# Reading the relative-position tables two units ahead, in pairs of batches

## The reference, cut to what matters

```python
q, k, v = heads(x @ Wq + bq), heads(x @ Wk + bk), heads(x @ Wv + bv)
pos_k = heads(rel_embeddings @ Wk + bk)              # 128 distance buckets
scores = q @ k.T
scores += take(q @ pos_k.T, bucket(i - j))           # c2p
scores += take(k @ pos_k.T, bucket(j - i)).T         # p2c
ctx = softmax(scores / sqrt(48)) @ v
out = layernorm(ctx @ Wo + bo + x) * ln_scale + ln_bias
```

## Time and profile before

| | us |
|---|---|
| median of 3 runs | 2724.37 (2719.42 to 2726.56) |
| the profiled execution's own time | 2727.48 |
| its span, first to last instruction | 2725.4 |
| granted TensorE clock, mean of the span | 0.847 of full |
| PE busy | 1965.8 (72%) |
| DVE busy | 1632.0 (60%) |
| ACT busy | 1046.4 (38%) |
| POOL busy | 898.0 (33%) |
| DMA, queue 1 (SP's) packets | 269344 packets, 398.77 MB |

### The profile page before, as it was taken

The page is one execution under the profiler, slowest core; times in us unless marked ns, Lnnn a source line. Parts: engine busy times, 40 slices in busy tenths (PEclk is TensorE's granted clock), DMA queues, the critical chain, the costliest instruction groups (busy, mean ns, idle before and its releaser), DMA issues. The chain is left out here.

```text
span 2725.4 us, 47318 instructions
## 1 busy us (share of the span) xinstructions
PE 1965.8 (72%) x13556; PEld 1445.9 (53%) x13557; DVE 1632.0 (60%) x4103; ACT 1046.4 (38%) x2098; POOL 898.0 (33%) x1079
## 2 busy tenths in 40 slices
PE   6867777777777777777769999755335159999742
PEld 3435666666666666665646666433225028877421
DVE  8946665666666566665765553577747754444344
ACT  3445554555555555555423223332001163333000
POOL 4122222222222222222232220267630015554656
PEclk9979898998988888888979999777565559999876
DMA  4679998998999899999742110000001414447333
GB/s 149 195 238 287 278 290 262 290 280 271 284 266 281 255 281 269 276 280 282 233 122 62 48 30 1 0 0 0 0 19 47 178 32 155 154 148 139 109 97 110
DMA packets 290039, 456.40 MB, mean 167 GB/s; under 512 B 38608, under 2 KB 225024, under 8 KB 289824
## 3 DMA queue, kind: packets, MB, share of 16 engines
q1 hardware_dynamic: 269344, 398.77, 48.6%
q0 software_dynamic: 16320, 42.39, 6.3%
q10 hardware_dynamic: 4160, 12.58, 1.2%
HBM read 236.67 MB, written 216.92 MB: 166 GB/s over the span
## 5 line engine op out<-in xcount | busy, mean ns | idle before, releaser
L935 DVE CUSTOM_DVE_ANT_0 probs<-bank,c2p 128x512 f32<-128x512 f32 x512 | 351.8, 687 | 425.7 <-PE bank L832 217.9
L893 ACT ACTIVATE probs<-probs,neg_max 128x512 f32<-128x512 f32 x512 | 371.5, 726 | 69.9 <-DVE neg_max L935 69.5
L908 ACT COPY a_stage<-bank 128x320 f32<-128x320 f32 (+1 forms) x512 | 211.9, 414 | 427.1 <-PE bank L801 416.3
L944 DVE COPY probsT<-bank 128x512 f32<-128x512 f32 x512 | 351.2, 686 | 11.0 <-PE bank L842 10.6
L842 PE MATMUL bank<-ident,probs 128*128 128x128 f32 x2048 | 334.7, 289 | 1.0 <-ACT probs L893 0.9
L813 PE MATMUL bank<-tab,k 96*128 96x320 bf16 (+1 forms) x512 | 165.0, 322 | 197.1 <-DVE b_stage L887 149.6
L842 PEld LDWEIGHTS bank<-ident,probs 128*128 128x128 f32 x2048 | 277.3, 152 | 13.1 <-issue 1.8
L771 POOL COPY end_c2p<-a_stage 128x4 f32<-128x4 f32 (+1 forms) x128 | 24.8, 194 | 752.0 <-ACT a_stage L908 596.9
L2122 POOL DMA_INDIRECT p_x_tile<-y_d,p_token x160 | 153.0, 956 | 329.4 <-POOLq L1813 207.4
L832 PE MATMUL bank<-ident,p2c 128*128 128x128 f32 x1280 | 249.1, 296 | 0.0
L827 PE MATMUL bank<-k,q 96*128 96x384 bf16 (+1 forms) x512 | 167.3, 327 | 91.7 <-DMA p2c<-p2c_d 66.2
(11 more groups left out here) (254 smaller groups left out, 3770.0 us busy)
## 6 DMA issues: line engine op xcount, KB each, us to landing
p2c_d<-b_stage SPq DMA_DIRECT2D x64, 640.0 KB, 4.9
c2p_d<-a_stage SPq DMA_DIRECT2D x64, 640.0 KB, 4.5
p2c_d<-b_stage SPq DMA_DIRECT2D x64, 576.0 KB, 5.2
c2p_d<-a_stage SPq DMA_DIRECT2D x64, 576.0 KB, 3.5
p2c<-p2c_d SPq DMA_DIRECT2D x256, 144.0 KB, 4.5
c2p<-c2p_d SPq DMA_DIRECT2D x256, 144.0 KB, 4.3
o_sorted_d<-p_o_pair SPq DMA_DIRECT2D x80, 256.0 KB
k<-k_stack_d SPq DMA_DIRECT2D x192, 64.0 KB
```

Source lines behind the costliest of these rows:

```text
L893: act.activation(probs[:, w % 2, j, :], probs[:, w % 2, j, :], ACT.Exp, bias=neg_max[:, w % 2, j:j + 1], scale=-1.0).then_inc(exp_done, 1)
L908: act.copy(staged(a_stage, wa % 2, wa % TPB)[:, j, :], bank[A_BANK][:, 0:width(wa % TPB)]).then_inc(a_copied, 1)
L935: dve.tensor_tensor_reduce(probs[:, w % 2, j, :], bank[S_BANKS[(HB * w + j) % 3]][:], c2p[:, w % 2, j, :], -SCALE, LOWEST, ALU.add, ALU.mi ...
L944: dve.tensor_copy(probsT[:, wp % 2, j], bank[T_BANKS[j % 2]][:].rearrange("p (k q) -> p k q", k=TPB)).then_inc(probsT_copied, 1)
```

## The change

The tables' four sequences are stored as two pairs (r) with the two members (e) of a pair alternating element by element, in the stage buffers, in HBM, and in the c2p and p2c tiles: [b, x] becomes [r, x, e]. A skewed read then takes runs of 320 to 576 floats, half as many. The copies into the stage buffers write every second element, DVE's add and PE's stationary load read every second element, and POOL's fills write pairs. c2p gets four buffers; its reads are issued directly behind the p2c reads of the same unit, two units ahead, and A_LEAD becomes 4. POOL's c2p fill waits for the adds of a unit one earlier. SP waits, ahead of the write of table A, for the c2p read of four units before. To make room, rows3, w1 and the second half of the row sums are no longer held beside stage 2: they are loaded at the start of stage 3, with waits there.

```diff
-        rsum_in = sb(early3, "p3_rsum", [P, 2, CC, S], side="right")
+        first_sums = sb(early3, "p3_first_sums", [P, CC, S], side="right")
...
-        w1 = sb(early3, "p3_w1", [P, CC, FFN], side="right")
-        rows3 = sb(early3, "p3_rows", [P, 4, C], side="right")
...
-        A_LEAD, B_LEAD = 3, 4
+        A_LEAD, B_LEAD = 4, 4
...
-            return stage[:, u, 0:HB * width(t)].rearrange("p (b x) -> p b x", b=HB)
+            return stage[:, u, 0:HB * width(t)].rearrange("p (r x e) -> p r x e", r=HB // 2, e=2)
...
-            c2p = sb(st, "c2p", [P, 2, HB, S])
+            c2p = sb(st, "c2p", [P, TPB, HB // 2, S, 2])
-            p2c = sb(st, "p2c", [P, TPB, HB, NEAR])
+            p2c = sb(st, "p2c", [P, TPB, HB // 2, NEAR, 2])
...
+            WEIGHTS3 = [(wo[:], a["wo"].rearrange("(c p) n -> p c n", p=P)), (b1[:], a["b1_col"]), (scale[:], row("scale"))]
...
                     def read_skewed(table_d, slot, t, dest, left, done):
                         for g in range(P // ROWS):
                             j0, j1 = varied(t, g)
-                            start = slot * P * HB * TABLE + ROWS * g * HB * width(t) + ROWS - 1 - ROWS * g - first_col(t)
-                            skew = bass.AP(table_d.tensor, start + j0,
-                                           [[HB * width(t) - 1, ROWS], [width(t), HB], [1, j1 - j0]])
-                            sp.dma_start(dest[g * ROWS:(g + 1) * ROWS, :, j0 + left:j1 + left], skew).then_inc(done, 16)
+                            start = slot * P * HB * TABLE + ROWS * g * HB * width(t) + 2 * (ROWS - 1 - ROWS * g - first_col(t))
+                            skew = bass.AP(table_d.tensor, start + 2 * j0,
+                                           [[HB * width(t) - 2, ROWS], [2 * width(t), HB // 2], [1, 2 * (j1 - j0)]])
+                            sp.dma_start(dest[g * ROWS:(g + 1) * ROWS, :, j0 + left:j1 + left, :]
+                                         .rearrange("p r x e -> p r (x e)"), skew).then_inc(done, 16)
...
-                        (i2, w2), (i1, w1) = ahead(i, w, 2), ahead(i, w, 1)
+                        i2, w2 = ahead(i, w, 2)
                         if is_unit(i2, w2):
-                            kt = w2 % TPB
+                            t = w2 % TPB
                             sp.wait_ge(b_written[w2 % 2], 16 * (BODY // 2 * i2 + w2 // 2 + 1))
                             apart(sp)
                             sp.wait_ge(p2c_filled, BODY * i2 + w2 + 1)
-                            read_skewed(p2c_d, kt, kt, p2c[:, kt], 0, p2c_loaded[kt])
-                        if is_unit(i1, w1):
-                            t = w1 % TPB
-                            sp.wait_ge(a_written[w1 % 2], 16 * (BODY // 2 * i1 + w1 // 2 + 1))
+                            read_skewed(p2c_d, t, t, p2c[:, t], 0, p2c_loaded[t])
+                            sp.wait_ge(a_written[w2 % 2], 16 * (BODY // 2 * i2 + w2 // 2 + 1))
                             apart(sp)
-                            sp.wait_ge(c2p_filled, BODY * i1 + w1 + 1)
-                            read_skewed(c2p_d, w1 % 4, t, c2p[:, w1 % 2], (t - 1) * P, c2p_loaded[w1 % 2])
+                            sp.wait_ge(c2p_filled, BODY * i2 + w2 + 1)
+                            read_skewed(c2p_d, t, t, c2p[:, t], (t - 1) * P, c2p_loaded[t])
...
                         if is_unit(ia, wa):
+                            wait_count(sp, c2p_loaded[wa % TPB], 64 * (4 * ia + wa // TPB))
...
-                            return pool.tensor_copy(dest[:, :, c0:c1], ends_of[:, side, :].unsqueeze(2).broadcast_to(
-                                [P, HB, c1 - c0]))
+                            pairs = ends_of[:, side, :].rearrange("p (r e) -> p r e", e=2)
+                            return pool.tensor_copy(dest[:, :, c0:c1, :],
+                                                    pairs.unsqueeze(2).broadcast_to([P, HB // 2, c1 - c0, 2]))
...
-                            wait_count(pool, scores_added, HB * n)
-                            pool.wait_ge(a_ends_copied, BODY * i1 + w1 + 1)
+                            left = (t - 1) * P
+                            wait_count(pool, scores_added, HB * (n - 1))
+                            pool.wait_ge(a_ends_copied, BODY * i2 + w2 + 1)
...
-                            last = pe.matmul(sc[:, kt * P:(kt + 1) * P], p2c[:, kt, j, (t - kt + 1) * P:(t - kt + 2) * P],
+                            last = pe.matmul(sc[:, kt * P:(kt + 1) * P], p2c[:, kt, j // 2, (t - kt + 1) * P:(t - kt + 2) * P, j % 2],
...
-                    copy(staged(b_stage, w % 2, w % TPB)[:, j, :], bank[B_BANK][:, 0:width(w % TPB)]).then_inc(copied, 1)
+                    copy(staged(b_stage, w % 2, w % TPB)[:, j // 2, :, j % 2], bank[B_BANK][:, 0:width(w % TPB)]).then_inc(copied, 1)
...
-                                    probs[:, w % 2, j, :], bank[S_BANKS[(HB * w + j) % 3]][:], c2p[:, w % 2, j, :],
+                                    probs[:, w % 2, j, :], bank[S_BANKS[(HB * w + j) % 3]][:], c2p[:, w % TPB, j // 2, :, j % 2],
...
+                    sp.dma_start(rows3[:, 0, :], row("bo")).then_inc(rows_loaded, 16)
                     load_in(0, 0)
+                    for k, name in ((1, "ln_scale"), (2, "ln_bias"), (3, "b2")):
+                        sp.dma_start(rows3[:, k, :], row(name)).then_inc(rows_loaded, 16)
+                    for c in range(CC):
+                        heads = slice(c * H // CC, (c + 1) * H // CC)
+                        sp.dma_start(rsum_in[:, 1, c], ctx_d[heads, 1:2, D:2 * D, :].rearrange("h b d s -> h (b d) s")
+                                     ).then_inc(next_loaded, 16)
                     sp.dma_start(sums[:], ctx_d[:, :, D, :]).then_inc(sums_loaded, 16)
+                    sp.dma_start(w1[:], a["w1T"].rearrange("(c p) n -> p c n", p=P)).then_inc(w1_loaded, 16)
...
+                        if isinstance(b, int) and b == 0:
+                            pool.wait_ge(rows_loaded, 16 * 4)
                         pool.tensor_tensor(n_bo[:], n_in[:, u], across(0), ALU.add).then_inc(n_bo_ready, 1)
...
+                        if isinstance(b, int) and b == 0:
+                            dve.wait_ge(w1_loaded, 16)
```

More of the change, by code:

```diff
@@ L614, in build @@
             a_written = [sem("a_written0"), sem("a_written1")]
-            c2p_loaded = [sem("c2p_loaded0"), sem("c2p_loaded1")]
+            c2p_loaded = [sem(f"c2p_loaded{k}") for k in range(TPB)]
             b_made = sem("b_made")
@@ L722, in step @@
                                     heads = slice(c * H // CC, (c + 1) * H // CC)
-                                    for dest, rows in ((ctx_in, slice(0, D)), (rsum_in, slice(D, 2 * D))):
-                                        sp.dma_start(dest[:, u, c], ctx_d[heads, u:u + 1, rows, :]
+                                    for dest, rows in ((ctx_in[:, u, c], slice(0, D)), (first_sums[:, c], slice(D, 2 * D)))[:2 - u]:
+                                        sp.dma_start(dest, ctx_d[heads, u:u + 1, rows, :]
                                                      .rearrange("h b d s -> h (b d) s")).then_inc(first_ctx_loaded[u], 16)
@@ L728, in _ @@
                         sp.wait_ge(ctx_written[g], 16 * UNITS // TPB // 2)
-                    sp.wait_ge(first_ctx_loaded[1], 16 * 2 * CC)
+                    sp.wait_ge(first_ctx_loaded[1], 16 * CC)
                 @block.gpsimd
@@ L754, in step @@
                             last.then_inc(p2c_filled, 1)
-                        if is_unit(i1, w1):
-                            t, left = w1 % TPB, (w1 % TPB - 1) * P
-                            lo, hi = near_tiles(t)
-                            wait_count(pool, scores_added, HB * n)
-                            pool.wait_ge(a_ends_copied, BODY * i1 + w1 + 1)
+                            left = (t - 1) * P
+                            wait_count(pool, scores_added, HB * (n - 1))
+                            pool.wait_ge(a_ends_copied, BODY * i2 + w2 + 1)
                             apart(pool)
                             for side, c0, c1 in constant(t):
-                                last = fill(c2p[:, w1 % 2], end_c2p[:, w1 % 4], side,
+                                last = fill(c2p[:, t], end_c2p[:, t], side,
                                             0 if side == 0 else c0 + left, S if side else c1 + left)
@@ L770, in copy_ends @@
                             apart(pool)
-                            pool.tensor_copy(ends_of[:, w % 4, ends(t), :].rearrange("p s b -> p b s"),
-                                             staged(stage, w % 2, t)[:, :, end_cols(t)]).then_inc(copied, 1)
+                            pool.tensor_copy(ends_of[:, w % 4, ends(t), :].rearrange("p s (r e) -> p r s e", e=2),
+                                             staged(stage, w % 2, t)[:, :, end_cols(t), :]).then_inc(copied, 1)
                         if is_unit(ia, wa):
@@ L907, in step @@
                                     wait_count(act, a_ends_copied, m - 1)
```

(11 more changed lines are left out.)

9 lines of the change are left out of this document (3 added, 6 removed).

## The result

The changed kernel takes 2762.68 us (median of 4 runs, 2758.16 to 2763.08) against 2725.47 for the kernel before in the same session: ratio 1.0132, interval 1.0105 to 1.0159. It is slower by 1.3%, where 2.2% faster was forecast (60 us). Its profiled execution has a span of 2756.4 us, 31.0 more than before.

A forecast was written before the change was run, and what follows sets the result against it. Stage 2 was taken to be bound by DMA transfers, lateness costing time only through DMA gaps. Terms of -43, -12, -4 and -1 sum to -60 us: 2667.5 for the profiled execution, 2664 against the median, range 2585 to 2712.

The forecast's parts named there:

- term 1: Stage 2, c2p read two units ahead: DVE's 176.2 us wait goes and DMA gaps close, -43 us.
- At nothing: Parts of the change counted as 0 us: A_LEAD 4, SP's new wait, POOL's fills, strided operands and PE's stationary load.
- a sign of being wrong: Stage 2's DMA share staying at 0.94 or below, where 0.97 or more was to show the forecast right.
- The best window of 100 us: Stage 2's fastest of eleven windows, taken as its pace with gaps closed: 8.82 us per unit for 9.16.
- the wait only changes its name: Rival, stage 2: p2c, loop ends and the b_stage copy hold DVE instead, share stays 0.94; 2708 us, chance 0.12.
- Term 2: Stage 2's table reads: half as many packets of twice the length read 2% faster, -12 us.
- The strong rival: Packet length matters strongly for stage 2's reads, which reach about 290 GB/s; 2600 us, chance 0.27.
- The estimate of 14 us: Stage 2's reads: 512 fewer packets per unit at a fixed three cycles each, 0.11 us per unit.
- Term 3: Loads moved to stage 3: -5.5 us from stage 2's last loop body, +1.5 at stage 3's start, net -4.
- The slow rival: PE's stationary load from p2c at 8-byte steps costs double, deciding from 64 ns more a load; 2799 us, chance 0.10.
- The 0 for ACT's strided copy: Stage 2: strided operands were taken to cost DVE and ACT nothing, 0 us.

The follow-up runs named there:

- j_early_loads: The change with every quarter of q and k loaded one step earlier (nine units ahead, not eight): 2704.36 us, ratio 0.9934 to the kernel before.
- k_lead1_early_loads: a_pairs_lead1 with the loads of q and k one step earlier: 2714.72 us, ratio 0.9964 to the kernel before.
- b_lead2_nopairs: The change with every pair undone, all else as changed: 2761.75 us, ratio 1.0139 to the kernel before.
- n_early_nopairs: j_early_loads with the pairs undone: 2705.71 us, ratio 0.9922 to the kernel before.
- q_early_rows_nopairs: n_early_nopairs with the row bo awaited alone at n_bo in stage 3: 2704.79 us, ratio 0.9922 to the kernel before.
- r_early_rows_c2p_pairs: q_early_rows_nopairs with table A and c2p in pairs: 2707.54 us, ratio 0.9929 to the kernel before.
- a_pairs_lead1: The change with c2p read one unit ahead again and A_LEAD 3, pairs and moved stage 3 loads kept: 2716.75 us, ratio 0.9975 to the kernel before.
- h_lead1_c2p_pairs: a_pairs_lead1 with only table A and c2p paired: 2693.44 us, ratio 0.9998 to the kernel before.

## Why the prediction was wrong

**The step that failed** is in term 1, where it says what comes when c2p's wait is gone: "Late next: p2c, which keeps its lead, and the b_stage copy." The loads of q and k are not among them, though PE already waited 29.2 us for q. Next to c2p's lateness that wait cost nothing (1.0002 without it); with c2p out of the way most of it counts. With A_LEAD 3 it is 38.4 us, and removing it takes the kernel from 1.0104 to 0.9969; in the change it is 70.6 us, and removing it takes the kernel from 1.0132 to 0.9934 and gives stage 2 back 61 us.

The step was made worse by one under "At nothing": "A_LEAD 4: the same PE and ACT work, a unit earlier; it wants q no earlier than table B does." It wants it in the same step, but as the second thing in it: behind one batch of scores, where table B comes behind the transposes too. The wait is 70.6 us there for 38.4, ahead of both tables. In time A_LEAD 4 cost 0.6% with c2p one ahead (0.9975 to 1.0035); two ahead the difference, 1.0104 to 1.0132, is within the intervals.

**Term 1 (-43 us)** had the right first half: c2p's wait went to nothing, and p2c is the longest wait for a read behind it. The second half, that the gaps in DMA close with it, failed, and the share at or below 0.94 that was named as a sign of being wrong came. SP begins a step only when PE has made the scores of the unit before, so it issues nothing while PE is held. Its own waits for ACT's copy of table A, which follows PE, show it: 85.0 us in the change, 48.5 before, 15.9 in j_early_loads. Even with q's waits gone, the second unit of lead at A_LEAD 3 is worth nothing (0.9964 and 0.9969); with A_LEAD 4 stage 2 is 16.5 us shorter than in k_lead1_early_loads (0.9964 and 0.9934 in time, intervals that overlap), the share is the 0.94 of before, not 0.97, and p2c takes over (173.6 us). The best window of 100 us was no measure of what removing one wait of several brings. The rival "the wait only changes its name", with 0.12, had it that new waits take c2p's place and that the share does not rise; it did not name q either, and its price was wrong in sign, as it took the new waits to be no dearer than the old.

**Term 2 (-12 us).** The rate of reads in the short windows rose to 238 GB/s from 231, 3% for the 2% taken. Over the window of 1100 us GB/s divided by the DMA share is 299 in the change (269 at 0.90) and 292 in b_lead2_nopairs (269 at 0.92), also 2%. So the size of the rate held; in time nothing of it shows in three comparisons (b_lead2_nopairs with the change, n_early_nopairs with j_early_loads, q_early_rows_nopairs with r_early_rows_c2p_pairs). The strong rival (0.27), which wanted some 290 GB/s, is out. The rate of these reads into 32 partitions hardly moves with the length of their packets: by the Trainium skill, SBUF — State Buffer, "Door 1: The DMA port swizzle (why [64,N] ≈ [32,N])", that is what should happen, and the trace agrees: 227 to 238 GB/s at shares of 1.07 to 1.15, or 197 to 222 for a share of 1, where the page has about 218. The estimate of 14 us from the Trainium skill, DMA: Bandwidth & Descriptors, "Why small descriptors are slow (HBM only)", is not borne out in time by any run here.

**Term 3 (-4 us).** Its part at the start of stage 3, +1.5, was +5.4 at n_bo, inside the stated end of +8; the sum left out that the diff has POOL wait for all four rows. Its other part, -5.5 for the loads that left stage 2, no run takes by itself: a_pairs_lead1 and h_lead1_c2p_pairs, which have it together with pairs, have a stage 2 that is 11.6 and 7.2 us shorter than before. w1 was hidden, as said: no wait for it is among the waits of stage 3.

**The slow rival** had the right side and the wrong mechanism. The load cost 52 ns more, under the 64 ns from which by its own working it was to decide; the runs agree (0.9975 with the slow load). The 0 for ACT's strided copy was 25 ns, without effect.

## What to carry to other kernels

A wait that a wait list shows as small may be small because a larger one runs beside it. Before removing the larger, ask of each transfer that lands in the same step when it was issued and when it is first wanted after the change, and give the next-latest its lead in the same edit. And when a producer is moved a step earlier, look at where it stands within its step: its inputs are wanted earlier by that too.

## What was not expected of the hardware

- PE's stationary load of 128x128 float32 elements at an 8-byte step takes 208 ns, against 156 at 4 bytes: a third more, not double, and hidden here. DVE's add with one operand at an 8-byte step takes 686 ns for 687, ACT's copy that writes every second element 439 for 414 (mean of 288 and 320 columns).
- Skewed reads into 32 partitions ran at 227, 231 and 238 GB/s with packets of about 700, 1030 and 1860 B, in windows of 1.2 us with shares of 1.15, 1.08 and 1.07.
